# Second expert stage: where the activation's result lives, and which engine rounds it

## The reference

```
proj = x @ Wp.T ; gate_scores = l2norm(proj) @ l2norm(sim_matrix).T / temperature
top_v, top_i = top_k(gate_scores, 2);  comb = one_hot(top_i) * softmax(top_v)
h   = gelu(x @ W1[e] + b1[e])        # 256 -> 1024, for each expert e
eo  = h @ W2[e] + b2[e]              # 1024 -> 256
out = sum over e of comb[., e] * eo
x   = x + tanh(g_ffn[1]) * out
```

## Time and profile before

| | |
|---|---|
| runs | 2302.42, 2302.52, 2305.07 us; median 2302.52 |
| profiled execution | span 2283.1 us from the first to the last instruction; the page gives no other time of it |
| TensorE busy in it | 1726.4 us (76%), weight loads 1464.7 (64%) |
| VectorE | 1157.5 us (51%) |
| ScalarE | 736.6 us (32%) |
| GpSimd | 726.0 us (32%) |
| L1716, the subtraction to `hidden_lo` | 136 times, 154.3 us busy, mean 1135 ns |

### The profile page before, as it was taken

The page is one execution under the profiler, slowest core; times in us unless marked ns, Lnnn a source line. Parts: engine busy times, 40 slices in busy tenths (PEclk is TensorE's granted clock), DMA queues, the critical chain, the costliest instruction groups (busy, mean ns, idle before and its releaser), DMA issues. The chain is left out here.

```text
span 2283.1 us, 42887 instructions
## 1 busy us (share of the span) xinstructions
PE 1726.4 (76%) x13667; PEld 1464.7 (64%) x13668; DVE 1157.5 (51%) x3147; ACT 736.6 (32%) x1397; POOL 726.0 (32%) x626
## 2 busy tenths in 40 slices
PE   3788888888677477745887887888563889887887
PEld 3677777777466355534565666665442888886887
DVE  3554454444166333334545545543265666667664
ACT  2343343443266111101444434444232222222221
POOL 4121111110077555552111111110276633334332
PEclk9898898898798699985889989998756899998989
DMA  4322332331222365643323223221522233323322
GB/s 115 96 84 78 95 89 74 88 82 47 68 84 102 103 109 108 109 94 99 94 84 100 77 79 101 73 64 41 190 83 72 67 72 78 73 69 69 74 34 39
DMA packets 166672, 191.72 MB, mean 84 GB/s; under 512 B 15442, under 2 KB 146868, under 8 KB 166324
## 3 DMA queue, kind: packets, MB, share of 16 engines
q1 hardware_dynamic: 135092, 149.69, 22.6%
q0 software_dynamic: 28416, 40.03, 9.7%
q10 hardware_dynamic: 3072, 0.79, 0.2%
HBM read 113.73 MB, written 75.67 MB: 83 GB/s over the span
## 5 line engine op out<-in xcount | busy, mean ns | idle before, releaser
L653 ACT ACTIVATE a_probs<-a_scores_t 128x384 f32<-128x384 f32 (+1 forms) x512 | 269.6, 545 | 427.6 <-PE a_scores_t L814 222.7
L1760 ACT ACTIVATE e_hidden<-e_h,t_up_bias 128x256 f32<-128x256 f32 x348 | 146.0, 470 | 557.6 <-PE e_h L1794 557.5
L557 DVE TENSOR_REDUCE a_row_max<-a_scores 128x2 f32<-128x512 f32 x256 | 170.9, 687 | 168.3 <-PE a_scores L799 166.7
L1809 PE MATMUL e_y_bank<-e_down_hi,e_hidden_hi 128*128 128x256 f32 x544 | 165.3, 304 | 67.2 <-DVE e_hidden_lo L1716 66.7
L1685 POOL DMA_INDIRECT out_rows<-e_y,e_token x68 | 113.2, 1664 | 308.5 <-DVE e_y L1743 289.0
L419 POOL TENSOR_TENSOR a_rest<-a_qk,a_parts 128x1024 f32<-128x1024 f32 x32 | 68.0, 2124 | 434.0 <-ACT a_parts L590 434.0
L554 DVE TENSOR_REDUCE a_row_max<-a_scores 128x1 f32<-128x128 f32 x256 | 73.2, 286 | 196.5 <-PE a_scores L796 195.3
L1809 PE MATMUL e_y_bank<-e_down_hi,e_hidden_lo 128*128 128x256 f32 x544 | 160.4, 295 | 0.0
L1809 PE MATMUL e_y_bank<-e_down_lo,e_hidden_hi 128*128 128x256 f32 x544 | 160.0, 294 | 0.0
L1794 PE MATMUL e_h<-e_xs_hi,e_up_hi 128*128 128x256 f32 x544 | 155.7, 286 | 2.1 <-DVE e_xs_lo L1706 2.0
L1809 PEld LDWEIGHTS e_y_bank<-e_down_hi,e_hidden_hi 128*128 128x128 f32 x544 | 111.3, 205 | 70.9 <-DVE e_hidden_lo L1716 70.7
(11 more groups left out here) (263 smaller groups left out, 4694.6 us busy)
## 6 DMA issues: line engine op xcount, KB each, us to landing
parts_dram<-a_parts SPq DMA_DIRECT2D x32, 768.0 KB, 4.1
e_xs_rows<-routed_rows_dram SPq DMA_DIRECT2D x76, 258.0 KB, 3.0
a_q_stack<-parts_dram SPq DMA_DIRECT2D x64, 192.0 KB
a_k_stack<-parts_dram SPq DMA_DIRECT2D x64, 192.0 KB
a_ctx_rows<-in_ctx SPq DMA_DIRECT2D x32, 256.0 KB, 11.1
a_q_stack<-parts_dram SPq DMA_DIRECT2D x64, 128.0 KB
a_k_stack<-parts_dram SPq DMA_DIRECT2D x64, 128.0 KB
t_up<-in_L_ffn_W SPq DMA_DIRECT2D x8, 1024.0 KB, 5.2
```

Source lines behind the costliest of these rows:

```text
L557: nc.vector.reduce_max(row_max[:, :, h], bank[:].rearrange("p (c t) -> p c t", c=TC), AX_X).then_inc(maxed, 1)
L653: nc.scalar.activation(probs[h % NP][:, 0:width], scores_t[h % 2][:, 0:width], ACT.Exp).then_inc(probs_ready, 1)
L1760: nc.scalar.activation(hidden[:, fc, :], h_bank[g][:, at:at + TS], act_func, bias=routed.up_bias[:, bass.ds(e * FC + fc, 1)]).then_inc(hid ...
L1809: last = nc.tensor.matmul(y_bank[:, c * D:(c + 1) * D], x[:, fc, c * P:(c + 1) * P], w[:, fc, :], start=(fc == 0 and term == 0), stop=(fc ...
```

## The change

The activations write their result back into the PSUM bank that they read, the SBUF tile `hidden` is gone in this stage, ScalarE rounds each bank to `hidden_hi` with one copy of 128x512 after its two activations, and VectorE only subtracts, from the bank. `need(act, y_done, t)` keeps ScalarE from overwriting `hidden_hi` while the down matmuls of the tile before still read it. The first expert stage (`split` false) keeps its form.

```diff
-        hidden = sb("hidden", [P, FC, TS])
+        hidden = None if split else sb("hidden", [P, FC, TS])
...
             def cut_hidden(t):
                 for g in range(N_BANKS):
-                    dve.wait_ge(hidden_ready, FC * t + (g + 1) * PER_BANK)
-                    src, hi, lo = (x[:, g * PER_BANK:(g + 1) * PER_BANK, :] for x in (hidden, hidden_hi, hidden_lo))
-                    nc.vector.tensor_copy(hi, src).then_inc(hidden_hi_done, 1)
+                    hi, lo = (x[:, g * PER_BANK:(g + 1) * PER_BANK, :].rearrange("p k s -> p (k s)") for x in (hidden_hi, hidden_lo))
                     dve.wait_ge(hidden_hi_done, N_BANKS * t + g + 1)
-                    nc.vector.tensor_tensor(lo, src, hi.bitcast(F32), ALU.subtract).then_inc(hidden_cut, 1)
+                    nc.vector.tensor_tensor(lo, h_bank[g][:], hi.bitcast(F32), ALU.subtract).then_inc(hidden_cut, 1)
...
         @block.scalar
         def _(act):
+            def round_hidden(t, g):
+
+                if g == 0:
+                    need(act, y_done, t)
+                act.wait_ge(hidden_ready, FC * t + (g + 1) * PER_BANK)
+                nc.scalar.activation(hidden_hi[:, g * PER_BANK:(g + 1) * PER_BANK, :].rearrange("p k s -> p (k s)"),
+                                     h_bank[g][:], ACT.Copy).then_inc(hidden_hi_done, 1)
+
...
-                    nc.scalar.activation(hidden[:, fc, :], h_bank[g][:, at:at + TS], act_func,
+                    out = h_bank[g][:, at:at + TS] if split else hidden[:, fc, :]
+                    nc.scalar.activation(out, h_bank[g][:, at:at + TS], act_func,
                                          bias=routed.up_bias[:, bass.ds(e * FC + fc, 1)]).then_inc(hidden_ready, 1)
+                    if split and fc % PER_BANK == PER_BANK - 1:
+                        round_hidden(t, g)
```

## The result

The changed kernel takes 2238.07 us (median, 2235.14 to 2245.16) against 2302.47 for the kernel before in the same comparison: the medians are 64 us apart, and the ratio of the comparison is 0.973 (0.971 to 0.9751), which is 62 us. On a second chip the same pair gave 2214.93 against 2286.38, 0.9699 (0.9674 to 0.9723). The median of the kernel before lies anywhere from 2286 to 2302 by chip and session, so ratios are what to compare. Two of the 13 executions of the kernel before on the second chip were slow (2329.76 and 7355.68 us); ratios and intervals leave them out. The forecast, 2233 from 2302.5, is 0.970.

The account below looks back on a forecast made before the run. TensorE sets the pace in the second expert stage, idle mainly while waiting for `hidden_lo`. Terms -66.7 - 16.5 + 13 + 3 - 2 = -69.2 us take 2302.5 to 2233 us; range 2212 to 2268.

Parts of the forecast that it names:

- The seven waits, -66.7: Second expert stage: TensorE's seven waits for `hidden_lo`, behind subtractions held up by GpSimd's weight cuts, vanish; 66.7 us gained.
- The slow matmuls behind them, -16.5: Down matmuls after the seven long waits, slowed by TensorE's halved clock, return to 5.76 us per 48; 16.5 us gained.
- The wait behind the `weight` copy, +13: At six weight cuts VectorE's small SBUF copy waits for GpSimd, making the next tile's low part late; 13 us lost.
- A gap of this size costs no clock: TensorE's remaining wait of about 2.2 us behind each of six cuts would leave its granted clock at 1.00.
- ScalarE, +3: ScalarE's rounding copies leave 0.25 us slack per tile; tiles that miss it cost 3 us over 34 tiles.
- small waits, -2: VectorE does one operation per bank instead of two, taking back 2 of 4.0 us of TensorE's small waits.
- In-place activations: ScalarE's activations writing the PSUM bank they read: bounds 0.42 and 0.70 us each, 0.47 taken.
- The 19.4 us around the span as fixed: The runs' median, 2302.5 us, exceeds the profiled span, 2283.1, by 19.4 us, assumed unchanged by the change.
- Rival B: VectorE's small copies slip past GpSimd's hold at the weight cuts: 13 us less, 2220 us; chance 0.16.
- C: ScalarE is late in each tile of the second expert stage: 2255 or 2283 us; chance 0.14.
- D: The new subtraction still waits for GpSimd, so the seven waits and the clock stay: 2302 us; chance 0.07.
- E: Slower: table loads at each change between Gelu and Copy, two of 1.28 us per bank: 2570 us; chance 0.06.

Follow-up runs that it names:

- (3): Kernel before, with VectorE instead of GpSimd subtracting the low weight parts; 2240.42 us, ratio 0.979 to the kernel before.
- (2): Changed kernel, but VectorE still rounds, both rounding and subtracting from the PSUM bank; 2242.13 us, ratio 0.980 to the kernel before.
- (1): Changed kernel, with ScalarE rounding but activations, rounding and subtraction all kept in SBUF; 2277.94 us, ratio 0.996 to the kernel before.
- Experiment 7: Changed kernel, with the copies of `weight` and `token` put ahead of the same tile's subtractions; 2196.76 us, ratio 0.9597 to the kernel before.
- experiment 9: Changed kernel, with ScalarE's rounding copy of each bank run twice, the first into a spare tile; ratio 0.9891 to the kernel before.
- the doubled hold: Changed kernel, with GpSimd's two subtractions at each weight cut run twice; 2289.81 us against 2214.93 for the changed kernel on that chip.

## Why the prediction was right

The second stage is the place to add up: 499.0 us before, 430.3 in the second profile of the change, which has the fast first tile as the kernel before has; -68.7, forecast -69.2. The terms measured -65.9, -16.5, +16.6 and, for the tiles with no cut, about -3; the forecast had -66.7, -16.5, +13 and +1. That the sums agree to 0.5 us is luck: two terms are off by nearly 4 us each, with opposite signs. The mechanism of the two large terms is what was right.

- *The seven waits, -66.7.* Right: 66.7 to 0.8 us (2.2 in the first profile). The reason is shown from both sides. Taking away GpSimd (3) or letting VectorE read the bank (2) ends them, taking away VectorE's roundings (1) does not. The reading of the trace was wrong in one of the seven: at the first cut the rounding was held and not the subtraction, so a second SBUF input is not needed for the wait. One instance in another stage had been enough to forecast it.
- *The slow matmuls behind them, -16.5.* Right for the seven, but see the next point but one.
- *The wait behind the `weight` copy, +13.* Right in mechanism and nearly in size, incomplete in the last link. The copy lasts 6.56 us, the six tiles behind a cut wait 11.5 us in all, forecast 13. The forecast let the next low part be the last to come and the row load land in time, by half a microsecond (0.4 us). The row load came later than that, and the two arrived together: the transposition is done at 1877.71, the low part is there at 1877.79. The row load alone, on time, would therefore have saved next to nothing at this cut. Experiment 7 removes the whole wait, but it moves both at once, so it does not tell what either is worth.
- *"A gap of this size costs no clock".* Wrong. It rested on gaps in a stage with slower rhythm. Behind three of the six gaps in the first profile of the change, two in the second, the clock fell, and the 48 down matmuls behind those gaps took 7.2 to 7.5 us, where nothing much over 6 was forecast. Here is the stretch behind the gap that ends at 1877.05 (same columns as above):

```profile
1877.70:1881.50 3.80, 3.66 (x19) 3.65 (x19) 3.32 (x8) 0.00 (x0) 1.31 (x1) 0.55 0.63 69
2005.40:2010.00 4.60, 4.54 (x37) 4.54 (x38) 3.24 (x8) 0.00 (x0) 1.22 (x1) 1.00 0.49 55
```

  The second row is behind a gap of 1.63 us in the same profile, at full clock. The tiles with the fall take 15.7 to 15.8 us, the others 13.9 to 14.5: about 1.5 us each. With the waits, the six tiles cost 16.6 us over 11.97 in the second profile, where +13 stood.
- *ScalarE, +3, small waits, -2.* The undisturbed tile is 11.97 us, so +3 was nothing; the small waits went entirely (-4), and the tiles of 12.3 that the kernel before has here and there went with them. The margin is as thin as said: a bank costs 0.81 + 0.03 + 0.60 = 1.44 us against TensorE's 1.44, and experiment 9 shows what is beyond it. In-place activations came at 444 ns, near the lower bound of 420; the row taken was 470. The Trainium skill, page "ScalarE: Activation LUTs", section "Step-by-step: what each stage is for", says that PSUM is ScalarE's lower-latency destination, and the trace agrees by 26 ns a piece.
- *The 19.4 us around the span as fixed.* Wrong, without effect on the difference. In all later runs an execution is 1.7 us longer than its span. By that the profiled execution of the kernel before took about 2285 us, 17 less than any of the three runs shown; this is an estimate, since its own time is not on record. The forecast in absolute terms rode on the median, which was right to do.

Rival B (copies slip past), C (ScalarE late), D (no release) and E (table loads) each fell to one row: the copy of 6.56 us, the tile of 11.97, the subtraction's maximum of 0.69, the one table load.

The Trainium skill, page "SBUF — State Buffer", section "Who interferes with whom", speaks of one exclusive lock on a shared port pair. The runs here agree: the new subtraction has a maximum of 694 ns in 136, in the doubled hold 693; subtractions with two SBUF inputs (10.4 and 10.6 us), the rounding within SBUF (9.5) and small copies within SBUF (6.6, 8.9, 16.0) end with GpSimd's.

## What to carry to other kernels

When an operation's maximum is many times its median, look at what the other engines do in those microseconds before counting work: reading the bank instead of SBUF, taking GpSimd away, or moving two tiny copies gave 46, 48 and 12 to 23 us here without removing arithmetic. After such a fix list every operation of the same kind that still falls into the hold, however small, who waits behind it, and whether the hold is shorter than the distance to the next one. An engine that is busy for 43% of a stage can be at its limit within a phase: compare its work per bank with the rhythm at which banks come.

## What the runs showed of the hardware that was not expected

- A copy of two elements per partition, 159 ns by itself, waited up to 16.0 us for GpSimd, and everything queued on VectorE with it.
- A rounding of 128x512 from SBUF to SBUF, one input, 0.42 us by itself, was held for 9.46 us just as the subtractions with two were.
- The same kernel's gaps of 1.6 to 2.0 us in TensorE brought its clock to 1.2 GHz in some cases (0.55 granted behind one) and not in others (1.00); what decides between them no run here shows.
- The first tile of the second expert stage takes 13.6 to 14.7 us or 20.5 to 21.5: the long form in all four profiles of one chip and the first profile of the change, the short one in all others, with the same kernel on both sides twice. Its cause was not tried.
